# A recurrent stack at batches of eight steps: attention in row form, the up projection cut by columns, and semaphores raised by one

## What is computed

```python
x = x + attention(x, cond)      # 16 heads, two keys only: a learned one and one made of cond
x = x + moe(x, cond)            # shared SiLU unit, plus the best 2 of 8 GELU experts
x = x + (gelu(cond @ Wp + b) @ W_u + x @ W_e)
x = x + lstm(x, h0=cond)        # below

def step(h, c):                 # xz = x @ Wx + b, h is (2, 256)
    z = xz_t + h @ Wh
    ai, af, ao, ag = split(z, 4)
    c = sigmoid(af) * c + sigmoid(ai) * tanh(ag)
    h = sigmoid(ao) * tanh(c)
```

## Time and profile before

| | us |
|---|---|
| runs: median of 3 (lowest, highest) | 1956.87 (1956.83, 1959.16) |
| the profiled execution, its own time | 1957.56 |
| its span, first to last instruction | 1955.8 |
| busy: PE matmul / weight loads / DVE / ACT / POOL | 1889.5 / 1439.8 / 1390.7 / 827.2 / 1133.8 |
| mean granted TensorE clock | 0.996 of full |

### The profile page before, as it was taken

One profiled execution on the slowest core, in us unless ns is written; L12 is line 12 of the kernel. 1 busy time (PEld: TensorE's weight loads), 2 busy tenths in 40 slices (PEclk: granted clock), 3 DMA queues, 4 the chain that ended last, 5 costly groups with the idle time before them and its releaser, 6 DMA issues.

```text
span 1955.8 us, 256304 instructions
## 1 busy us (share of the span) xinstructions
PE 1889.5 (97%) x113680; PEld 1439.8 (74%) x113680; DVE 1390.7 (71%) x7217; ACT 827.2 (42%) x4757; POOL 1133.8 (58%) x4950
## 2 busy tenths in 40 slices
PE   7999999999999999999999999999999999999998
PEld 5777777777777777777777777777777777777776
DVE  2677777777777777777777777777777777777776
ACT  1344444444444444444444444444444444444444
POOL 4555655655555565565555556555555655665565
PEclk9899999999999999999999999999999999999999
DMA  4000000000000000000000000000000000000000
GB/s 170 4 4 3 3 4 3 3 3 4 3 3 4 3 3 3 4 3 3 4 3 3 4 3 3 3 4 3 3 4 3 3 3 4 3 3 4 3 3 3
DMA packets 57724, 14.67 MB, mean 8 GB/s; under 512 B 56176, under 2 KB 56304, under 8 KB 57200
## 3 DMA queue, kind: packets, MB, share of 16 engines
q1 hardware_dynamic: 57712, 14.50, 3.2%
HBM read 12.37 MB, written 2.10 MB: 7 GB/s over the span
## 4 chain that ended last, share of the span: by engine, by line
PE 87%; ACT 6%; DVE 4%; issue 2%; DMA 0%; POOL 0%; DVEq 0%; SPq 0%; POOLq 0%; ACTq 0%
PE psum L953 29%; PE psum L943 29%; PE psum L815 10%; PE psum L836 7%; PE psum L855 6%; DVE h_ring L703 3%; ACT o_act L532 3%; ACT psum L535 2%; PE psum L798 2%; PE psum L829 2%; PE psum L843 1%; PE psum L892 1%; PE psum L793 0%; DMA wkv_sb<-in_wkv 0%; PE psum L776 0%
## 5 line engine op out<-in xcount | busy, mean ns | idle before, releaser
L943 PEld LDWEIGHTS psum<-wh_sb,h_ring 128*2 128x2 f32 (+1 forms) x32768 | 488.4, 90 | 416.6 <-DVE h_ring L703 409.8
L953 PE MATMUL psum<-h_ring,wh_sb 128*32 128x2 f32 x65536 | 765.7, 173 | 1.8 <-issue 1.8
L953 PEld LDWEIGHTS psum<-h_ring,wh_sb 128*32 128x32 f32 x65536 | 725.8, 109 | 2.0 <-issue 2.0
L943 PE MATMUL psum<-wh_sb,h_ring 128*2 128x64 f32 (+1 forms) x32768 | 656.8, 220 | 50.8 <-DVE h_ring L703 20.2
L526 ACT ACTIVATE f_act<-psum 128x4 f32<-128x4 f32 x1024 | 177.3, 173 | 698.6 <-DVE psum L744 698.6
L744 DVE STREAM_TRANSPOSE psum<-psum 128x64 f32<-128x64 f32 x1024 | 266.1, 260 | 274.6 <-PE psum L943 262.7
L815 PE MATMUL psum<-up_sb,x 128*32 128x256 f32 (+1 forms) x3096 | 311.8, 460 | 0.0
L746 DVE STREAM_TRANSPOSE psum<-psum 128x64 f32<-128x64 f32 x1024 | 271.5, 265 | 1.9 <-PE psum L943 1.9
L703 DVE SCALAR_TENSOR_TENSOR h_ring<-o_act,psum 128x4 f32<-128x4 f32 x1025 | 163.0, 159 | 141.9 <-ACT psum L535 115.9
L836 PE MATMUL psum<-down_e,hid_t 128*16 128x256 f32 x3096 | 251.6, 382 | 0.6 <-ACT down_e L507 0.6
L756 DVE TENSOR_TENSOR_SCAN psum<-addend,psum 128x16 f32<-128x16 f32 x1024 | 199.3, 195 | 52.2 <-ACT psum L529 2.4
(11 more groups left out here) (142 smaller groups left out, 2286.0 us busy)
## 6 DMA issues: line engine op xcount, KB each, us to landing
x_a<-in_x SPq DMA_DIRECT2D x129, 16.0 KB, 1.6
x_s<-in_x SPq DMA_DIRECT2D x129, 16.0 KB, 1.6
up_sb<-in_up SPq DMA_DIRECT2D x1, 2048.0 KB, 12.7
out_y<-y_sb SPq DMA_DIRECT2D x128, 16.0 KB, 1.4
down_sb<-in_down SPq DMA_DIRECT2D x1, 1536.0 KB, 8.3
wx_sb<-in_wx SPq DMA_DIRECT2D x1, 1024.0 KB, 14.5
wh_sb<-in_wh SPq DMA_DIRECT2D x1, 1024.0 KB, 16.6
wkv_sb<-in_wkv SPq DMA_DIRECT2D x1, 512.0 KB, 4.4
```

The lines of the kernel that those rows point to most:

```text
L943: last = nc.tensor.matmul(z[32 * j:32 * j + row + B, :], h_ring[:, prev, c, WIN - B - row:WIN], wh_v[:, c, g, j, :], start=False, stop=(c ...
L953: last = nc.tensor.matmul(by_row(z)[32 * j:32 * (j + 1), m, row:row + B], wh_v[:, c, g, j, 32 * m:32 * (m + 1)], h_ring[:, prev, c, WIN - ...
```

## The change

Three things are changed together.

1. `attend` has the mask (now 32 columns wide, its right part zero) as the stationary operand and the values as the moving one, in four pieces of 64 columns, each for 32 output partitions. The result lies in rows, so DVE transposes it (`turn_attention`, into `attn_t` in SBUF, in step 6), and `attended` reads it from there with a wait for `attn_turned`.
2. The up projection's product of the first half of the rows with the second expert's columns (`EXPERT_1`, 128 of 512) moves from after step 5 to after step 2, behind `down_mm(1)` and a wait for `w1_out`. It comes first now and so carries the start flag; the part after step 4 no longer does.
3. Semaphores of a batch's work rise by one. The loops count batches (`i`), `batch` is the value to wait for, and t is worked out from i for the recurrence's counters. `hid` becomes eight semaphores, one for each step of the batch, on which PE waits with `batch` as well.

```diff
-            def attend(attn, weights):
-                for c in range(C):
-                    for j in range(0, P, 64):
-                        last = nc.tensor.matmul(attn[j:j + 64, c], value_w[:, c * P + j:c * P + j + 64], weights,
-                                                start=True, stop=True, skip_group_check=True)
+            value_v = value_w[:, :].rearrange("p (c j m) -> p c j m", c=C, j=J)
+            def attend(attn, weights):
+                for j in range(J):
+                    last = nc.tensor.matmul(attn[32 * j:32 * (j + 1), :], weights, value_v[:, :, j, :],
+                                            start=True, stop=True, skip_group_check=True)
...
+            def turn_attention(up_to):
+                nc.vector.transpose(attn_t[:, :, :].rearrange("p c t -> p (c t)"), attn_b).then_inc(attn_turned, up_to)
...
             dve.wait_ge(attn_made, 1)
-            attended(x1_first, attn_first_b[:, :, 0, :], x_first[:, 0, :, :])
+            nc.vector.transpose(attn_first_t[:, :, :].rearrange("p c t -> p (c t)"),
+                                attn_first_b).then_inc(attn_turned, 1)
+            dve.wait_ge(attn_turned, 1)
+            attended(x1_first, attn_first_t[:, :, 0:NB], x_first[:, 0, :, :])
...
-            base_f(READY + U)
+            base_f(AHEAD + 1)
+            dve.wait_ge(attn_made, 2)
+            turn_attention(AHEAD)
...
-                                               op0=ALU.add, op1=ALU.mult).then_inc(hid, 1)
-            with dve.Fori(READY, READY + T, U) as t:
+                                               op0=ALU.add, op1=ALU.mult).then_inc(hid[(slot + 1) % U], 1)
+            with dve.Fori(0, BATCHES) as i:
+                t = dve.snap(i * U + READY)
+                batch = dve.snap(i + (AHEAD + 1))
                 now = t
...
                     elif u == 1:
-                        dve.wait_ge(x_ready, now)
-                        dve.wait_ge(stream_made, now)
-                        attended(x1, attn_b, x_a[:, :, :])
+                        dve.wait_ge(x_ready, batch)
+                        dve.wait_ge(stream_made, batch)
+                        dve.wait_ge(attn_turned, batch)
+                        attended(x1, attn_t[:, :, 0:NB], x_a[:, :, :])
...
+                    elif u == 6:
+                        dve.wait_ge(x1_out, batch)
+                        turn_attention(1)
...
-                    pe.wait_ge(hid, now)
+                    pe.wait_ge(hid[u], batch)
...
                     elif u == 2:
-                        pe.wait_ge(hid_e0t, now)
+                        pe.wait_ge(hid_e0t, batch)
                         down_mm(1)
+                        pe.wait_ge(w1_out, batch)
+                        up_mm(0, EXPERT_1, True, x1)
                     elif u == 3:
-                        attend(attn_b, w1_own[:, :]).then_inc(down_made, U)
+                        attend(attn_b, w1_own[:, :]).then_inc(down_made, 1)
                     elif u == 4:
-                        sum_mm().then_inc(x3_made, U)
-                        up_mm(1, SHARED, True, x1)
+                        sum_mm().then_inc(x3_made, 1)
+                        up_mm(1, SHARED, False, x1)
                     elif u == 5:
-                        up_mm(0, ALL, False, x1).then_inc(up_made, U)
+                        up_mm(0, BUT_EXPERT_1, False, x1).then_inc(up_made, 1)
```

More of the change, by code:

```diff
@@ L27 @@
 LEAD = 3
-READY = 2 * U
+AHEAD = 2
+READY = AHEAD * U
 J = 4
@@ L302, in cond_stack_kernel @@
         cell_tanh = sem("cell_tanh")
-        hid = sem("hid")
+        hid = [sem(f"hid_{u}") for u in range(U)]
         h_read = sem("h_read")
@@ L352, in _ @@
             pool.sem_inc(y_stored, 16)
-            for s in (f_made, i_made, o_made, f_turned, a_f, cell, cell_tanh, hid, x_turned, i_based):
+            for s in (f_made, i_made, o_made, f_turned, a_f, cell, cell_tanh):
                 pool.sem_inc(s, READY)
+            for s in (x_turned, i_based, *hid):
+                pool.sem_inc(s, AHEAD)
             pool.sem_inc(terms_in, 2 * READY)
             pool.sem_inc(i_and_c_in, 2 * READY)
-            pool.sem_inc(own_out, READY)
-            pool.sem_inc(w1_out, READY)
-            pool.sem_inc(h_read, READY + U)
+            pool.sem_inc(own_out, AHEAD)
+            pool.sem_inc(w1_out, AHEAD)
+            pool.sem_inc(h_read, AHEAD + 1)
             pool.memset(w1_own[:, :], 0.0).then_inc(cleared, 1)
@@ L516, in _ @@
                 take_fold(k)
[L517 to L521, removed]
+            act.wait_ge(hid_e_out, 1)
+            unit_acts(2)
+            take_partial(AHEAD, AHEAD)
+            with act.Fori(0, BATCHES) as i:
+                t = act.snap(i * U + READY)
+                batch = act.snap(i + (AHEAD + 1))
                 for u in range(U):
@@ L713, in _ @@
                     if u == 1:
-                        dve.wait_ge(h_read, now)
+                        dve.wait_ge(h_read, batch)
                     close((u - 1) % U)
@@ L748, in _ @@
                         dve.wait_ge(f_turned, now)
-                        dve.wait_ge(x_injected, now)
-                        base_f(U)
+                        dve.wait_ge(x_injected, batch)
+                        base_f(1)
                     dve.wait_ge(a_f, now)
@@ L975, in _ @@
                         stream_mm(x1)
-                        pe.wait_ge(hid_st, now)
-                        down_mm(0).then_inc(stream_made, U)
+                        pe.wait_ge(hid_st, batch)
+                        down_mm(0).then_inc(stream_made, 1)
                     elif u == 1:
-                        pe.wait_ge(x1_out, now)
+                        pe.wait_ge(x1_out, batch)
                         scores()
```

228 lines of the change are left out of this document (116 added, 112 removed).

## The result

The changed kernel takes 1947.59 us (median of 5 runs, 1946.10 to 1948.18), against 1956.87 before. The ratio on one chip is 0.9947, with an interval of 0.9937 to 0.9958. So it is faster by 9.3 us by the medians (10.4 by the ratio), where 18.7 had been forecast: the sign is right, the time lies inside the range, 0.4 us from its far end, and half of the gain is missing. The profiled execution took 1946.10 us (1957.56 before), with a span of 1944.3 us and a mean granted clock of 0.996.

The account below looks back on a forecast made before the run. The recurrence was taken to bound the kernel, with filler delaying three beats. -0.18 a pass times 127 (-22.9), loop head +3.8 and once +0.4 gave -18.7 us: 1938.2 us, range 1930 to 1948.

Parts of the forecast that it names:

- rival B: A new wait at L599, the loop head or `h_read` costs one uncovered operation, 11.5 us: 1945.9; two, 1953 or more; chance 0.12.
- The forecast's own band: Whole kernel: 1931 to 1943 us around the forecast of 1938.2, chance 0.75.
- What bounds the kernel: Eight-step loop: quiet beats are the recurrence; PE hides about 0.86 us of filler; three beats are late by 0.12, 0.06, 0.06.
- 1, `attend`: PE after step 3: row form with 32-column stationary tiles brings step 4's beat to 1.83, gaining 0.12 us a pass.
- Rival C: `attend`, after step 3: stall due to something else there, so 15.2 us don't come: 1953.4; chance 0.05.
- 2, the up projection: PE after steps 2 and 5: filler of 0.77 and 0.70 us, both hidden; step 6's beat gains 0.06 a pass.
- 3, the transpose: DVE, head of step 6: `turn_attention` takes 0.27 us, hidden in 0.60 us of idle time; cost 0.
- 4, the third wait: `attended` (L599), step 1, no cover: the added wait costs 0, bounds -0.03 and +0.09 us.
- 5, semaphores: Semaphores raised by one, `hid` in eight: vanishing instructions lie in idle time or beside matmuls; 0, at most 0.16 us gained a pass.
- 6, the loop heads: DVE, between a pass's last scan and the next first close: added register work, mostly covered, costs 0.03 us a pass.
- 7, POOL: Step 0's close against `half_h`: slack of 0.29 shrinks to 0.19, or 0.11 us; cost taken as 0.
- 8, once: Before the loop: two transposes add 0.4 us in all; the first pass changes by 0, bounds -0.5 to +0.5.

## Why the prediction was right, and where half of the gain went

The time of 1947.59 lies in the range of 1930 to 1948 only because that range also held the near part of rival B. The forecast's own band, 1931 to 1943, was missed, so the hit on the total was narrow and partly luck, while most of the parts were right.

*What bounds the kernel.* Right. The closes as beats, the filler's cover and the list of late beats all held; the quiet beat is 1.82 to 1.83 in every kernel.

*1, `attend`.* Right in size and cause: 0.12 was taken, 0.114 came (1.945 to 1.831), 0.115 alone. The stall belongs to the 64-column shape at this place, as the 32-column pieces show by curing it in the old form. Rival C is out. But a change of shape has no fixed price. `route` also leaves the 32-column shape, in the kernel before, and its load has no idle time marked:

```profile
1004.75 0.30 PEld L807 LDWEIGHTS psum<-route_t,small_sb 128*128 128x128 f32 x2
```

The matmuls ahead of it move 8 columns each, those ahead of `attend` 256. A stall that lasts until the matmuls ahead are nearly done would fit both rows; that is not tested.

*2, the up projection.* Right: 0.06 was taken, 0.060 came (1.895 to 1.835); 0.70 us were worked out for the piece after step 5, and it took 0.72. The piece after step 2 came to 0.71 rather than 0.77 and delayed nothing. But the step didn't ask what 16 more instructions do to PE's loop. In the kernel before they cost some 319 us; part 3 takes out seven additions, and with those gone the loop ran undisturbed. That "PE saves a register addition a step, beside running matmuls", priced at 0, is true of their time and misses what they are worth.

*3, the transpose.* Right: in step 6 the f transpose still had 0.38 us of idle time before it (the earlier trace rows had 0.60), as this row shows:

```profile
1007.14 0.27 DVE L768 STREAM_TRANSPOSE psum<-psum 128x64 f32<-128x64 f32 x1 [0.38 <-PE psum L970]
```

*4, the third wait.* Right: step 1 is 1.825 after, and 1.825 with `attend` alone.

*5, semaphores.* This is the step that failed: register work in the semaphore part was put at nothing, and it cost 0.089 us a pass. "None lies between two closes" was said of the instructions that vanish, and for them it was true. It was then used as if it covered all of part 3. The prediction didn't ask where `batch` is computed on DVE. The part on loop heads assumed that the work is all done at the head; but a value is computed where it is first used, and the first use lies between the wait for the tanh and the close. The price was on paper: 0.04 + 0.05 for an addition on the path, 0.089 measured. Alone and with DVE's head placed, part 3 costs 0.098 a pass, so the vanished semaphore instructions give nothing back, as was taken. Rival B had the kind and the size, one uncovered operation for 11.5 us and 1945.9 in all, at a chance of 0.12, and looked for it at L599, the head and `h_read`. It came at a fourth place, with 11.3, and the median lies 1.7 above B's time. (By its own sum B's figure for two such operations should be 1957.4, not 1953.)

*6, the loop heads.* 0.03 was taken and 0 came (step 7 is 1.885 in both). The cover was of unknown size: measured, the register work at the head ends 0.074 us before the tanh in the kernel before and 0.042 before it after, so the added operation fits. That the cost can sit in the code's placement was not seen; in the kernel with the semaphores alone it was 0.048 on step 7 and 0.038 on step 0.

*7, POOL.* Right in the result: `half_h` ended 0.46 before the close of step 0, or 0.37 without that close's own delay, where 0.11 to 0.19 were worked out. The 0.16 us of idle time ahead of L420 (now L428) are down to 0.08, and the rest of POOL's chain came earlier too.

*8, once.* Neither term can be read from these runs. The first close came 0.24 later where 0.4 was worked out, but it lies anywhere from 40.7 to 42.1 us in the runs without the two transposes, and from 42.2 to 42.7 in those with them (the placed heads aside). The first pass took 0.9 less, outside its bounds of 0.5; the kernel with `batch` early took 25.4 for it, 2.4 more than the kernel after, with the same matmuls.

The kernel with `batch` in a register early, at 1936.3, is what the forecast of 1938.2 described.

## What to carry to other kernels

When a wait's value is changed, look at where the sequencer computes it: a register operation between the last wait and the instruction that closes the critical loop takes over that wait and adds 0.09 us here, and one earlier use of the same value removes it. Before adding small instructions to an unrolled loop, look at the instruction queue's row and at how many instructions a pass has; each part of a change should be tried on its own too, since here one part was only possible because another made room. Price a beat by what comes between its last wait and its end, not by what an engine does in all.

## What the runs showed of the hardware that was not expected

- TensorE's loop had a longest length in this kernel. With 1,792 instructions a pass the instruction queue had 9 packets in the run (0.15 MB) and a pass took 14.74 or 14.79 us; with 1,798 it had 190 or 369 packets (3.11 or 6.05 MB), 20 or 40 passes loaded nine each and took 27.8 to 31.0 us, the mean granted clock of the profiled execution was 0.895 or 0.831, and the run was 16% or 27% longer. So the loss has two parts, the stalls and the half clock (0.50) that stretches behind them ran at. Why a pass of the same loop loads its instructions again while most of its neighbours don't, and why one of the two kernels did so twice as often, isn't settled.
- On DVE a wait ahead of a register operation goes with that operation. Of two waits with nothing between them, the second had a semaphore instruction of its own (21 ns, some 0.07 us on the path).
- The time from a loop's branch to its next instruction depended on where the loop lay: 0.19 to 0.20 us in most kernels, 0.27 in one. Placing the head brought 0.27 back to 0.20, for 2.5 us once.
